# Attention on one core: the last multiply of a head moves from VectorE to GpSimd, the maxima run six tiles ahead, the DMA queue is reordered, and layer 2's maximum products become pairs of 64 rows

## The reference, cut to what matters

```python
x = x + attention_with_relative_positions(groupnorm(x))     # layer 1: 12 heads of 32, scores + rel_h + rel_w
t = t + attention(layernorm(t))                             # layer 2: 12 heads of 32, no positions
t = t + mixture_of_experts(layernorm(t))                    # 8 experts, 2 for each token, hidden size 1536
# both attentions, for each head, over all 1024 keys:
attn = softmax(q @ k.T * scale (+ positions)); out = attn @ v; out = out @ w_proj.T + b_proj
```

## Time and profile before

| what | value |
|---|---|
| median of three runs | 1007.57 us (1000.21 to 1009.1) |
| the profiled execution | 1002.1 us, its span 1000.3 us |
| PE, PEld busy | 879.1 us (88%), 641.9 us (64%) |
| DVE, ACT, POOL busy | 526.9 us (53%), 328.3 us (33%), 457.2 us (46%) |
| layer 1's heads | 117.75 to about 332 us of the span |
| layer 2's heads | 412.02 to about 614 us |
| the experts | 684 to 937 us |

### The profile page before, as it was taken

How to read it: one execution, slowest core, us unless ns; L and a number is a source line. 1 busy time by engine, 2 the same in 40 slices (tenths; PEclk the granted TensorE clock), 3 DMA queues, 4 the chain that set the end, 5 groups by cost and what they waited for, 6 DMA issues and landing times.

```text
span 1000.3 us, 17750 instructions
## 1 busy us (share of the span) xinstructions
PE 879.1 (88%) x6029; PEld 641.9 (64%) x6030; DVE 526.9 (53%) x883; ACT 328.3 (33%) x582; POOL 457.2 (46%) x360
## 2 busy tenths in 40 slices
PE   4969899999998899999898978616999999999991
PEld 3457466566665444555454534516999999999991
DVE  4334767676776444878788772722233333233224
ACT  0212144554545222445454544201222322322230
POOL 0000076676778200346464665558076177077303
PEclk9989699999999999999999989957999999999996
DMA  9564723534424019335464571351356455455214
GB/s 291 109 147 150 271 76 87 130 104 110 127 84 154 11 32 231 92 84 176 127 206 126 195 241 37 125 185 49 115 179 219 145 174 197 167 181 176 87 32 141
DMA packets 74367, 139.23 MB, mean 139 GB/s; under 512 B 11000, under 2 KB 49080, under 8 KB 74320
## 3 DMA queue, kind: packets, MB, share of 16 engines
q1 hardware_dynamic: 62720, 120.42, 39.3%
q10 hardware_dynamic: 9552, 11.93, 3.6%
q0 software_dynamic: 2048, 6.29, 2.0%
HBM read 91.39 MB, written 43.55 MB: 135 GB/s over the span
## 4 chain that ended last, share of the span: by engine, by line
PE 43%; issue 8%; DVE 8%; POOL 6%; DMA 3%; ACT 1%; DVEq 0%; SPq 0%; POOLq 0%; ACTq 0%
PE ps L796 14%; PE ps L807 11%; DVE mhalf L891 4%; PE ps L628 4%; PE ps L585 3%; PE ps L603 3%; POOL qf L518 3%; PE ps L727 2%; PE ps L618 2%; POOL xs L547 1%; POOL gy L556 1%; PE ps L683 1%; DVE rec L901 1%; PE ps L778 1%; ACT prob L1074 1%
## 5 line engine op out<-in xcount | busy, mean ns | idle before, releaser
L891 DVE TENSOR_REDUCE mhalf<-ps 128x1 f32<-128x512 f32 x384 | 242.0, 679 | 95.6 <-PE ps L603 94.1
L1074 ACT ACTIVATE prob<-ps 128x1024 f32<-128x1024 f32 x192 | 190.5, 1026 | 186.7 <-PE ps L628 110.0
L518 POOL TENSOR_TENSOR qf<-qf,prob 128x1024 f32<-128x1024 f32 x84 | 206.1, 2453 | 18.2 <-POOL qf L518 8.1
L796 PE MATMUL ps<-xT,w 128*128 128x128 f32 x1440 | 166.8, 278 | 1.6 <-ACT xT L1146 1.4
L796 PEld LDWEIGHTS ps<-xT,w 128*128 128x128 f32 x1440 | 166.1, 194 | 2.1 <-issue 2.1
L603 PE MATMUL ps<-km,qm 96*128 96x512 f32 x384 | 145.3, 445 | 20.1 <-DVE mhalf L891 15.3
L618 PE MATMUL ps<-qa,ka 97*128 97x512 f32 x384 | 147.4, 426 | 8.6 <-DMA qa<-row 8.2
L1163 ACT ACTIVATE h_f<-ps,b1c 128x128 f32<-128x128 f32 x240 | 68.4, 368 | 215.6 <-PE ps L796 161.0
L603 PEld LDWEIGHTS ps<-km,qm 96*128 96x128 f32 x384 | 74.1, 194 | 71.5 <-DVE mhalf L891 51.9
L514 POOL TENSOR_TENSOR qf<-prob 128x1024 f32<-128x1024 f32 x24 | 57.1, 2379 | 134.7 <-ACT prob L1074 134.7
L628 PE MATMUL ps<-prob,va 128*32 128x256 f32 x1536 | 109.8, 393 | 0.0
(11 more groups left out here) (130 smaller groups left out, 874.5 us busy)
## 6 DMA issues: line engine op xcount, KB each, us to landing
w<-in_w SPq DMA_DIRECT2D x24, 768.0 KB, 7.4
w_raw<-in_w SPq DMA_DIRECT2D x24, 768.0 KB, 12.0
heads<-parts SPq DMA_DIRECT2D x56, 256.0 KB, 4.7
qa<-heads SPq DMA_DIRECT2D x24, 256.0 KB, 3.7
ka<-heads SPq DMA_DIRECT2D x24, 256.0 KB, 3.9
qb<-heads SPq DMA_DIRECT2D x12, 512.0 KB, 5.1
xs<-zero SPq DMA_DIRECT2D x8, 768.0 KB, 4.9
qm<-heads SPq DMA_DIRECT2D x12, 384.0 KB, 3.7
```

Of the source, the lines that this page charges most:

```text
L518: pool.tensor_tensor(acc[b], acc[b], prob[:, n % NP, :], ALU.add).then_inc(a_ok[L], 1)
L796: last = mm(ps[:, g, c % HG * P:(c % HG + 1) * P], w1[b][:, k, c * P:(c + 1) * P], xT[:, k, :], start=(k == 0), stop=(k == KT - 1))
L891: v.tensor_reduce(mhalf[:, b, qt, half:half + 1], max_bank(qt, half), AX.X, ALU.max).then_inc(mx_ok[L], 1)
L1074: act.activation(prob[:, s % NP, :], ps[:, 2 + 2 * (s % 2):4 + 2 * (s % 2), :].rearrange("p a b -> p (a b)"), ACT.Exp).then_inc(p_ok[L], 1)
```

## The change

Four edits, all in the two attentions:

1. **`output` moves from VectorE to GpSimd.** The multiply of a head's output with the reciprocals now stands in GpSimd's program behind the last add of the following head; for the last head behind that.
2. **`AHEAD` is 6.** The last two tiles of the next head are reduced at `s` = 0 and 1, the first six of the one after it at `s` = 2 to 7; the first head of a layer has two tiles at `s` = 0. `turn_max` stands behind step 2, `place_max` behind step 4.
3. **SyncE's order.** In the loop the output of head `h - 3` is stored, ahead of `load_a(h)`; one more store stands behind the loop.
4. **Layer 2's maximum products run on 64 rows**, the first half of the keys on rows 0 to 63 and the second on rows 64 to 127. For that, queries and the second half of the keys are loaded a second time at row 64 (two more DMAs for each head), and rows 96 to 127 of `qm` and `km` are cleared once, by four memsets at the program's start; two memsets at the end of layer 1 go.

```diff
-AHEAD = 5
+AHEAD = 6
...
-MAXIMA_FIRST = [[(1, 5)], [(1, 6)], [(1, 7)], [(2, 0)], [(2, 1)], [(2, 2)], [(2, 3)], [(2, 4)]]
+MAXIMA_FIRST = [[(1, 5), (1, 6)], [(1, 7)], [(2, 0)], [(2, 1)], [(2, 2)], [(2, 3)], [(2, 4)], [(2, 5)]]
...
-        qm = [put(f"qm{i}", [96, N], F32R) for i in range(2)]
-        km = [put(f"km{i}", [96, N], F32R) for i in range(2)]
+        qm = [put(f"qm{i}", [P, N], F32R) for i in range(2)]
+        km = [put(f"km{i}", [P, N], F32R) for i in range(2)]
...
                     sp.dma_start(f(km[b][0:HD, :]), rows(h, "K_HI")).then_inc(ld_m[L][b], 16)
+                    if L == 1:
+                        sp.dma_start(f(qm[b][64:96, :]), rows(h, "Q_HI")).then_inc(ld_m[L][b], 16)
+                        sp.dma_start(f(km[b][64:96, HALF:N]), rows(h, "K_HI")[:, HALF:N]).then_inc(ld_m[L][b], 16)
...
-                store(0, 0, 0)
                 with sp.Fori(0, (NH - 4) // 4) as q:
                     for n in range(4):
                         h = q * 4 + n + 3
                         load_m(h + 1, n % 2)
-                        load_a(h, 1 - n % 2)
                         if L == 1:
...
-                        store(h - 2, 1 - n % 2, n + 1, q)
+                        store(h - 3, n % 2, n, q)
+                        load_a(h, 1 - n % 2)
+                store(NH - 4, 0, NH - 4)
                 load_a(NH - 1, 1)
...
-                def add_tiles(h, b, last=False):
+                def output(h, b):
+                    pool.wait_ge(o_rc[L], 4 * (h + 1))
+                    wait(pool, st_o[L][b], 32 * (h - b))
+                    pool.sem_inc(pool_in, 1)
+                    pool.tensor_tensor(osb[b][:], vsb[:, 0, :], rec[:], ALU.mult).then_inc(o_ok[L], 1)
+
+                def add_tiles(h, b, first=False, last=False):
...
+                        if n == ADDS[L] and not first:
+                            output(h - 1, 1 - b)
+                    if last:
+                        output(h, b)
...
-                n_m, n_a = (2, 5) if L == 0 else (2, 4)
+                n_m, n_a = (2, 5) if L == 0 else (4, 4)
...
-                        mm(max_bank(qt, half), qm[b][0:96, qt * P:(qt + 1) * P],
-                           km[b][0:96, half * HALF:(half + 1) * HALF], start=True, stop=True).then_inc(sm_ok[L], 1)
+                        rows = slice(0, 96) if L == 0 else slice(64 * half, 64 * half + 64)
+                        mm(max_bank(qt, half), qm[b][rows, qt * P:(qt + 1) * P],
+                           km[b][rows, half * HALF:(half + 1) * HALF], start=True, stop=True).then_inc(sm_ok[L], 1)
...
                 v.memset(f(ka[i][96:104, :]), 1.0)
+                for wide in (qm, km):
+                    v.memset(f(wide[i][96:P, :]), 0.0).then_inc(wide_ok, 1)
...
-                def output(h, b):
-                    wait(v, st_o[L][b], 32 * (h - b))
-                    v.wait_ge(o_rc[L], 4 * (h + 1))
-                    v.tensor_tensor(osb[b][:], vsb[:, 0, :], rec[:], ALU.mult).then_inc(o_ok[L], 1)
-
...
-                        if s == 6 and not first:
-                            output(h - 1, 1 - b)
...
-                        for rows in (slice(32, 64), slice(64, 96)):
-                            v.memset(f(qm[i][rows, :]), 0.0).then_inc(wide_ok, 1)
+                        v.memset(f(qm[i][32:64, :]), 0.0).then_inc(wide_ok, 1)
```

More of the change, by code:

```diff
@@ L530, in _ @@
                 take_v(0, 0)
-                add_tiles(0, 0)
+                add_tiles(0, 0, first=True)
                 add_tiles(1, 1)
@@ L672, in first_maxima @@
                             else:
-                                pe.wait_ge(wide_ok, 4)
+                                pe.wait_ge(wide_ok, 6)
                         max_scores(h, h, m)
@@ L938, in _ @@
                     invert_sums(NH - 1, part)
-                output(NH - 1, 1)
                 v.wait_ge(biased, L + 1)
```

## The result

The changed kernel takes 1011.15 us in the median of 12 runs (1008.59 to 1015.79); the kernel before took 1003.57 in 12 runs beside it. The ratio is 1.0080, with a 95% interval of 1.0057 to 1.0104. The forecast was 995 with a range of 982 to 1012: the time lies at the range's upper end, and the sign is wrong. The profiled execution after took 1009.79 us, its span is 1008.0.

The account below looks back on a forecast made before the run. Layer 1's heads were taken as TensorE-bound, layer 2's as stalled by VectorE's multiply waiting for GpSimd's add. Terms -17.6 - 1.7 + 1.5 + 4.3 + 1.5 - 3.5 + 8 = -7.5 us from 1002.1 gave 995, range 982 to 1012.

Parts of the forecast that it names:

- Six ahead: Each layer's first head: same products in another order, but a pair more there, +1.5 us.
- -3.5: Layer 2's end: the row's turn comes some 2 us earlier and that head's stall goes, -3.5 us.
- SyncE: DMA queue: two more DMAs a head, but the maxima's load no longer stands behind a multiply, 0.
- Multiply: Both attentions: off VectorE it ends layer 2's stall and layer 1's late loads; on GpSimd it costs +1.5 us.
- -17.6: Layer 2's heads three to ten: without the multiply's stall they fall from 138.1 us to 15.06 each, -17.6 us.
- -1.7: Layer 1: two TensorE waits, caused by the late multiply delaying SyncE's store and the next loads, go, -1.7 us.
- 0.79: GpSimd: estimated time in us of its 128x256 multiply, bounds 0.43 and 1.05.
- Rival C: Layer 2's heads: the stall turns into another, heads end near 16 us, -9.8 for -17.6, total 1002; chance 0.19.
- Pairs: Layer 2's maximum products on 64 rows: halves overlap but each visit pays at both ends, +8 us.
- Rival A: Layer 2's pairs cost no visit: weights load ahead and halves overlap, -3 instead of +8, total 984; chance 0.24.
- Rival B: Layer 2's 93 pairs: halves do not overlap, second starts 0.23 us behind, some 19 us more, total 1014; chance 0.14.
- Memsets: Program start: four more memsets ahead of the first norm, covered by nothing, shift everything to the end, +4.3 us.

Follow-up runs that it names:

- the run five ahead: The changed kernel with the maxima five tiles ahead again (second edit undone), everything else kept: 1001.96 us, ratio 0.9970 to the kernel before.
- keys first: The changed kernel with the fourth head's maximum operands loaded ahead of the third head's score operands: 1004.33 us, ratio 1.0005 to the kernel before.
- The best version with pairs: The best version plus the pairs on 64 rows, their memsets behind the norm: 993.99 us, ratio 0.9903 to the kernel before.
- best version: Changed kernel with 96 rows, fourth head's maximum operands loaded earlier, first head's extra tile made before it, two old memsets behind the norm: 983.67 us, ratio 0.9815.

## Why the prediction was wrong

**The step that failed** is "Six ahead. The same products in another order ... **+1.5**", with its "**-3.5**", and beside it "SyncE. ... the load for the maxima no longer stands behind a multiply. 0." Together -2; by the run five ahead the edit cost some 11 us. I looked at the order of the products on TensorE and at what follows in SyncE's loop, and not at the three loads ahead of the loop: there the fourth head's keys stand behind a load that waits for the first head's scores. Six ahead asks for these keys a step earlier, in both layers. The late keys account for some 7.5 us (keys first), a cost that the sum put at nothing.

The other part is the +1.5 itself, the extra pair in the first heads, which comes with a longer stretch at the slow clock there (20.5 us for 17.1 about layer 1's). The best version with pairs makes this pair ahead of the head: layer 1's first head then takes 17.16 us and layer 2's 13.72, where with the keys mended alone they take 20.03 and 19.70, some 9 us more together. In layer 1 all five kernels that have the pair inside the head take 19.5 to 20.0 for it, the eight others 17.1 to 17.9. Against both stands what six ahead gains by itself, some 5 us (best version). The end that I forecast for it is right: the wait of 5.49 is gone.

**Multiply.** Right in mechanism. Heads three to ten went from 138.1 to 126.4 with the pairs in them, and to 120.4 without: the -17.6 in full. On its own the edit gave 14: 15.8 in the eight heads, and the eleventh head of layer 1 gave 3.2 back. There the row comes 3.1 to 3.8 us late in all three kernels with GpSimd's multiply and five ahead, 0.7 to 0.9 late in three with VectorE's multiply, and the sum had no term for it. The -1.7 for layer 1's late loads came, from the queue's order. The 0.79 estimated for GpSimd is 0.73. One reading was off: behind the add VectorE's multiply took 0.28 us, not 0.43. Rival C is out.

**Pairs.** Right, +8 forecast; 9 to 10 in the mended kernel. A visit is 1.10 us for the 1.11 worked out from the visits to column groups. The Trainium skill, TensorEngine Tiling (Array Packing), section Key Properties, says that a change of tiling mode drains the engine. The trace agrees for row groups in so far as a visit costs more than like products (1.10 for 0.94); the drain itself is in no row.

Rival A fell: the halves overlap, with both products in 0.50 us, but the weights of a pair are not loaded ahead of it. The Trainium skill, TensorE: Matmul & The Clock Gate, section Part 3, says that weights for other row groups load ahead. The trace agrees inside a pair, whose halves start 3 ns apart; between a pair and the products of full height nothing was gained. Rival B was half right in its place: in 32 of the 64 pairs the second half waits for its bank. Its price was not paid: on 96 rows (best version) the second product starts 0.23 us or more behind the first in every one.

**Memsets.** +4.3 forecast; 3.6 to 3.8 measured at the norm's first product, because without them the norm soon waits for a DMA. It reaches the heads: the first starts at 121.8 to 123.4 in the five kernels with the memsets at the start, at 117.75 to 120.1 in all others.

**Not in any term:** the lower clock in new places. Every other kernel run here, those with one edit alone included, has in its one profile a stretch at 1.2 GHz in layer 1's projection that the one profile before does not have (3.4 us in the change); what brings it stays open. A slow stretch in layer 2's first heads came in the four kernels with pairs, six ahead and the extra tile inside the first head, and in no other; with five ahead, without pairs, or with the extra tile made earlier there was none. Why these three together bring it was not settled.

None of the rivals that I wrote down was the one that came. The slower one was built on the most visible new thing, the pair; the loss came from an edit that I had priced as a gain of 2 us. A slip in the chances besides: all of A and four tenths of the forecast are 0.41, not 0.43.

## What to carry to other kernels

When work is moved a step earlier, follow its operands back through the queue to the first time each is loaded, above all in the code ahead of a loop, and ask what wait stands in front of that load. Price an edit against the kernel as the other edits leave it: the same pairs cost 6.5 us while VectorE stalled and hid part of them, and 11 once it did not. A product that runs in halves side by side, alone between products of full height, pays for going in and coming out; here that was more than the overlap gave. Whether several such products in a row gain was not tried.

## What the runs showed of the hardware

A pair of products on 64 rows each, on different rows, starts 3 ns apart and takes 0.50 us, as long as one; two on the same rows take 0.66 from the first one's start to the next group's, of which the second starts 0.33 behind the first. Two on 96 rows among products of 97 rows take 0.48 (547.73 to 548.21). The 64-row products stand behind a change of row groups; a score product behind such a change also has the next one 0.34 behind it, so the 0.33 need not be the 64 rows' doing.

VectorE's multiply of 128x256 takes 0.43 at its shortest and 2.17 to 2.45 beside GpSimd's add; GpSimd's own takes 0.73.
